# P x V of a macaron block: the two array halves take one head each, and ScalarE alone empties the banks

## The reference

```
scores = jnp.einsum('bqhd,bkhd->bhqk', q_full, k_full) * softmax_scale
causal = jnp.tril(jnp.ones((S, S), dtype=bool))
scores = jnp.where(causal[None, None], scores, jnp.finfo(scores.dtype).min)
attn = jax.nn.softmax(scores, axis=-1)
out = jnp.einsum('bhqk,bkhd->bqhd', attn, v).reshape(B, S, H * VD)
return out @ wo.T
```

## Time and profile before

| what | value |
|---|---|
| runs | 1891.0, 1892.49, 1895.84 us (median 1892.49) |
| profiled execution, span | 1895.1 us |
| TensorE busy | 1803.7 us, 95% |
| VectorE busy | 1231.4 us, 65% |
| ScalarE busy | 1000.5 us, 53% |
| GpSimd busy | 877.8 us, 46% |
| attention's P x V (L1307) | first at 386.6 us, last at 1332.0 us |

### The profile page before, as it was taken

One profiled execution on the slowest core, in us unless ns is written; L12 is line 12 of the kernel. 1 busy time (PEld: TensorE's weight loads), 2 busy tenths in 40 slices (PEclk: granted clock), 3 DMA queues, 4 the chain that ended last, 5 costly groups with the idle time before them and its releaser, 6 DMA issues. The chain is left out here.

```text
span 1895.1 us, 44298 instructions
## 1 busy us (share of the span) xinstructions
PE 1803.7 (95%) x15472; PEld 1422.9 (75%) x15472; DVE 1231.4 (65%) x2654; ACT 1000.5 (53%) x2137; POOL 877.8 (46%) x641
## 2 busy tenths in 40 slices
PE   5999969899999999999999999998999999989999
PEld 4788869877777777777777777775788888877887
DVE  5655358688898888889888888989521111125453
ACT  2221047788887888888787888877310100112110
POOL 3232112377777878777787878775000000014321
PEclk9999979999999999999999999999999999989999
DMA  6542162311212112121222212123742233224321
GB/s 217 193 156 100 67 173 94 84 62 44 86 59 78 57 62 80 57 80 40 85 69 68 69 51 82 55 86 113 249 151 89 94 100 115 67 87 158 130 89 59
DMA packets 111969, 182.74 MB, mean 96 GB/s; under 512 B 27680, under 2 KB 64672, under 8 KB 109856
## 3 DMA queue, kind: packets, MB, share of 16 engines
q1 hardware_dynamic: 111904, 181.88, 29.8%
HBM read 122.33 MB, written 59.51 MB: 96 GB/s over the span
## 5 line engine op out<-in xcount | busy, mean ns | idle before, releaser
L1290 PE MATMUL psS<-keyT,q 128*128 128x512 f32 (+2 forms) x2304 | 473.2, 350 | 23.9 <-POOL q L648 14.5
L1290 PEld LDWEIGHTS psS<-keyT,q 128*128 128x128 f32 x2304 | 381.2, 189 | 118.2 <-DVE negmax L1408 41.7
L1357 ACT ACTIVATE prob<-prob,negmax 128x640 f32<-128x640 f32 (+7 forms) x512 | 392.0, 767 | 78.5 <-DVE negmax L1408 75.9
L1418 DVE STREAM_TRANSPOSE pT<-prob 128x640 f32<-128x640 f32 (+7 forms) x512 | 379.9, 762 | 66.4 <-PE psV L1307 61.6
L1408 DVE CUSTOM_DVE_ANT_0 prob<-psS,mask 128x640 f32<-128x640 f32 (+7 forms) x512 | 371.9, 742 | 20.9 <-PE psS L1290 7.4
L469 PE MATMUL f_psy<-f_weff,f_xT 128*128 128x512 f32 x1344 | 315.6, 393 | 0.0
L1101 PE MATMUL psS<-o_w,o_o 128*128 128x512 f32 x1344 | 304.8, 389 | 0.0
L469 PEld LDWEIGHTS f_psy<-f_weff,f_xT 128*128 128x128 f32 x1344 | 250.9, 188 | 55.8
L1101 PEld LDWEIGHTS psS<-o_w,o_o 128*128 128x128 f32 x1344 | 252.3, 188 | 52.4
L1307 PE MATMUL psV<-pT,val 32*64 32x512 f32 (+3 forms) x8192 | 264.8, 407 | 6.4 <-DVE pT L1418 6.2
L1307 PEld LDWEIGHTS psV<-pT,val 32*64 32x64 f32 x8192 | 168.8, 132 | 109.7 <-issue 66.2
(11 more groups left out here) (120 smaller groups left out, 1919.1 us busy)
## 6 DMA issues: line engine op xcount, KB each, us to landing
wo<-in_wo SPq DMA_DIRECT2D x16, 1024.0 KB, 6.0
pT<-row_scales SPq DMA_DIRECT2D x128, 128.0 KB, 2.9
oT<-pT SPq DMA_DIRECT2D x64, 256.0 KB, 2.5
o_in<-oT SPq DMA_DIRECT2D x32, 512.0 KB, 5.2
f_xt<-in_x SPq DMA_DIRECT2D x16, 512.0 KB, 4.4
f_w_in<-in_w SPq DMA_DIRECT2D x16, 512.0 KB, 6.7
w_sum<-f_w_in SPq DMA_DIRECT2D x16, 512.0 KB, 5.3
x<-f_xo SPq DMA_DIRECT2D x16, 512.0 KB, 3.0
```

The lines of the kernel that those rows point to most:

```text
L1290: ins = nc.tensor.matmul(psS[:, slot, start + x0:start + x1], q[:, e, a, t * P:(t + 1) * P], k.keyT[:, m, b * S + x0:b * S + x1], start=(i ...
L1357: nc.scalar.activation(row, row, ACT.Exp, bias=negmax[:, n % 8:n % 8 + 1], scale=-1.0, accum_out=rowsum[:, column(n, s):column(n, s) + 1]) ...
L1418: nc.vector.transpose(pT[:, n % 2, t, 0:width], prob[:, n % RING, 0:width]).then_inc(turned, 1)
```

## The change

TensorE: the two column halves now take the two heads (index e), and each half walks through all four key blocks. A matmul streams one head only, up to 8 x 32 = 256 columns, and there are 256 matmuls in a step instead of 128; each weight block is now loaded once for each head. The number of columns that each of the eight tiles streams is the same. A bank now holds finished sums, head 0 on partitions 0 to 63 and head 1 on 64 to 127, in 256 columns.

ScalarE: one copy of 128x256 per bank writes `o_raw` itself and raises `evicted`; it takes over the wait for the stores of the step before.

VectorE: the four O jobs are gone from `DVE_STEP`, the semaphore `copied` is gone, and the last round's `weights_lo` is one run over all 16 pairs.

```diff
-            "T6+0 R0+0 T7+0 O0-1 M8+0 O1-1 F0+0 M9+0 O2-1 T8+0 F1+0 M10+0 M11+0 T9+0 O3-1 M12+0 M13+0 T10+0 T11+0 "
+            "T6+0 R0+0 T7+0 M8+0 F0+0 M9+0 T8+0 F1+0 M10+0 M11+0 T9+0 M12+0 M13+0 T10+0 T11+0 "
...
-        def upper(bank):
-
-            return (cosT, sinT)[bank // 2][0:KVR, bank % 2 * BANK:(bank % 2 + 1) * BANK]
+        def of_block(bank):
+
+            return bank[:, 0:32 * QT].rearrange("p (t r) -> p t r", r=32)
...
-                for a in range(BLOCKS // 2):
-                    for half in range(2):
+                for block in range(BLOCKS):
+                    for e in range(2):
                         for i in range(BLOCKS):
-                            rows, block = slice(32 * i, 32 * i + 32), BLOCKS // 2 * half + a
-                            x = kt * P + 32 * block
-                            out = psV[KVR * half:KVR * half + KVR, i, :].rearrange("p (e t r) -> p e t r", e=2, r=32)
-                            ins = nc.tensor.matmul(out[:, :, kt:QT, :], val[rows, b, block, kt, :], pT[rows, :, kt:QT, x:x + 32],
-                                                   start=(kt == 0 and a == 0), stop=(kt == QT - 1 and a == BLOCKS // 2 - 1))
+                            rows, x = slice(32 * i, 32 * i + 32), kt * P + 32 * block
+                            out = of_block(psV[KVR * e:KVR * e + KVR, i, :])
+                            ins = nc.tensor.matmul(out[:, kt:QT, :], val[rows, b, block, kt, :], pT[rows, e, kt:QT, x:x + 32],
+                                                   start=(kt == 0 and block == 0), stop=(kt == QT - 1 and block == BLOCKS - 1))
...
                 if later(step, 1):
-                    act.wait_ge(evicted, step * 4 + bank - 3)
-                nc.scalar.activation(upper(bank), psV[KVR:P, bank, :], ACT.Copy).then_inc(copied, 1)
+                    for ch in range(2):
+                        act.wait_ge(o_stored[ch], step * 16)
+                nc.scalar.activation(by_block(o_raw, bank), of_block(psV[:, bank, :]).rearrange("p (h t) r -> p h t r", h=2),
+                                     ACT.Copy).then_inc(evicted, 1)
...
-                dve.wait_ge(copied, step * 4 + bank + 1)
...
-                    ins = nc.vector.tensor_tensor(by_block(o_raw, bank)[KVR * e:KVR * e + KVR], halves[0], halves[1], ALU.add)
-                ins.then_inc(evicted, 1)
...
-                        if r.last and s == 1 and n == 0:
-                            output.weights_lo(nc, dve, range(2 * SLOTS))
-                        join_values(r.it, n, s)
...
-            output.weights_lo(nc, dve, range(2 * SLOTS, PAIRS))
+            output.weights_lo(nc, dve, range(PAIRS))
```

More of the change, by code:

```diff
@@ L1134, in attention_phase @@
         r_stored, r_loaded = c.sem("r_stored"), [c.sem(f"r_loaded{ch}") for ch in range(2)]
-        valued, copied, evicted, scaled = c.sem("valued"), c.sem("copied"), c.sem("evicted"), c.sem("scaled")
+        valued, evicted, scaled = c.sem("valued"), c.sem("evicted"), c.sem("scaled")
         o_stored = [c.sem(f"o_stored{ch}") for ch in range(2)]
@@ L1431, in row_scales @@
                 nc.vector.transpose(rinvT[:, x // QT, :], rinv[:]).then_inc(r_turned, 1)
-            def join_values(it, bank, s):
-                step = it * 2 + s
-                dve.wait_ge(copied, step * 4 + bank + 1)
[L1437 to L1442, removed]
-                    ins = nc.vector.tensor_tensor(by_block(o_raw, bank)[KVR * e:KVR * e + KVR], halves[0], halves[1], ALU.add)
-                ins.then_inc(evicted, 1)
             nc.vector.memset(rinv[:], 1.0).then_inc(zeroed, 1)
@@ L1456, in body @@
                         row_scales(r.it, n, s)
-                    elif job == "O":
-                        if r.last and s == 1 and n == 0:
-                            output.weights_lo(nc, dve, range(2 * SLOTS))
-                        join_values(r.it, n, s)
                     elif job == "F":
```

## The result

The changed kernel takes 2218.5 us (median of 4 runs, 2201.8 to 2224.7), the kernel before in the same session 1893.6 (1891.0 to 1895.8): 1.170 times as long (95% interval 1.165 to 1.175). Forecast were 1930 us and at most 1960. The direction was right. The size was wrong by 288 us, nearly all of the loss.

The account below looks back on a forecast made before the run. TensorE, busy 95% of the span, was taken as the bound almost everywhere. 1895.1 us, plus 15 (26.0 - 3 - 3.1 - 4.5), plus 23 for refetched code, gave 1933 against the profiled span, so 1930 us; range 1898 to 1960.

Parts of the forecast that it names:

- Pace of the pairs: TensorE's P x V: each pair of weight load and matmul takes at least 14.5 ns, making P x V 1.4 us longer.
- the floor: TensorE's P x V: a least time per pair, 14.5 ns, so 0.93 us for the 64 pairs of a narrow key tile.
- The reading of kt 7: Old trace's narrowest key tile: 0.61 us, some 0.2 of it the last matmul's way, leaving 12.5 ns a pair.
- The forecast that kt 4 to 7 would be alike: The four narrow key tiles of P x V: each takes 0.85 to 1.0 us, whatever its columns.
- Waits behind P x V vanish: TensorE's waits on GpSimd and VectorE right behind P x V: mean 0.6 us a step, absorbed by the longer P x V.
- VectorE, ScalarE and the last steps: Joins gone: 3 us gained over the steps, 3.1 in the last two steps, 4.5 behind the last P x V.
- The new wait of ScalarE for the stores: ScalarE's copy waits for the stores of the step before: costs nothing; up to 2.5 us a step if uncovered.
- The body doesn't stay in the store: TensorE's loop body, grown to 2465 records, over ten packets, is fetched again at returns; held likelier than that it fits.
- Price of a return: TensorE's loop head, right behind P x V: 1.8 us per refetch, 13 returns, 23 us; range 1.0 to 3.5 a return.
- Packets inside P x V: TensorE's P x V: forecast 9.3 to 9.9 us long, with some 150 instruction packets on q8 in the run.
- rival 3: Fetches inside P x V on demand only: two steps lose 14 us more, the kernel passes 2100 us; chance 0.05.
- Rival 2: P x V grows only 0.1 us, swallowed by the waits behind it: 1885 us; not slower below 0.9 us growth; chance 0.1.

Follow-up runs that it names:

- experiment 6: The kernel before with only its last 1, 2, 4 or 5 key tiles written one head at a time: 1898.2, 2000.5, 2105.4, 2161.9 us.
- Experiment 2: The kernel before with ScalarE copying whole 128x256 banks and VectorE joining nothing, TensorE untouched, some sums and columns left out: 1883.4 us, ratio 0.994.
- Experiments 3: The kernel before with two rounds written out in TensorE's loop body, 2977 records, seven passes in place of 14: 1944.9 us, ratio 1.026.
- experiment 4: The changed kernel with TensorE's 16 rounds written out, so without any return to a loop head: 2151.1 us, ratio 1.139 against the kernel before.
- Experiment 5: The kernel before with TensorE's 16 rounds written out, so without any return to a loop head: 1897.7 us, ratio 1.0017.
- experiment 7: P x V of key tiles kt 0 to 3 left out of the changed kernel and of the kernel before: 1955.5 and 1957.5 us.

## Why the prediction was wrong, point by point

**Pace of the pairs (14.5 ns, +1.4 us per P x V): too high, and not what counted.** With the code at hand 64 pairs take 0.65 to 0.70 us where the floor gave 0.93, and the four narrow tiles grow by 0.68 us where 1.4 was forecast (3.71 + 0.25 against the 2.57 of the earlier trace rows). The reading of kt 7 was sound: the trace has 0.22 us for the last matmul's way, as allowed, and so some 12.5 ns a pair. The step from there up to 14.5 failed, the argument that a long run of narrow parts has less queued: four such parts on end go at 14.7, 12.3, 10.9 and 10.2 ns, the later the faster. The forecast that kt 4 to 7 would be alike fell as well: 0.94, 0.79, 0.70, 0.65.

**Waits behind P x V vanish (0.6 us): right, though a P x V as long as this one makes it certain.** In the changed kernel's list of waits TensorE has one on GpSimd left, of 0.5 us, where before there were 44 with 14.5 us. With one tile apart (experiment 6) P x V grows by 0.29 us (first to last start 8.28 against 7.99) and the kernel by only 4 us, 0.13 a step: the waits took the other half, so at a small growth not all of the 0.6 us comes back.

**VectorE, ScalarE and the last steps (-3 and -7.6 us): right by themselves, nothing of it in the changed kernel.** Experiment 2 carries them alone. From the second P x V to the one before the last it gains 3.9 us over 29 steps, 0.14 a step against 0.1. The last step gave 1.6 where 3.1 was forecast, and behind the last P x V 6.6 us where 4.5 was. The terms forecast add up to 10.6 and the median moved by 10.3; two of them missed by half in opposite directions, so that match is partly luck. In the changed kernel 573.7 us follow the start of the last P x V, before they were 573.0: two waits for packets inside it, 5.5 us, took its place. The new wait of ScalarE for the stores cost nothing, and its copy takes 389 ns:

```profile
L1372 ACT ACTIVATE pT<-psV 128x256 f32<-128x256 f32 x128 | 38.8, 389 | 231.5 <-PE psV L1306 231.5
```

The row gave 382. The 231.5 us of idle time ahead of it show the copies now waiting for P x V, so nothing of ScalarE is on the path.

**The body doesn't stay in the store: right**, and the sentence "nothing says that the store is much larger than what it was seen to hold" bore it out. The edge lies between 1617 and 1745 records. (The 2465 records of the prediction are matmuls and weight loads alone; the body has 2513.) The Trainium skill, "Runtime: NRT & Kernel Launch", section "Instruction fetch mechanics", gives TensorE 2048 instructions, refilled first in, first out. By it alone 1745 and 2001 records would stay, and experiment 6 does not agree: 42 packets against 98 put the edge lower. Whether the store is smaller, or a part of it goes to what is read past the loop's end, no run tells.

**Price of a return (1.8 us, bounds 1.0 to 3.5): mis-sized, the first failed term.** The wait is 4.3 us in the mean (56.1 / 13), beyond the upper bound. It was built from a small DMA's way and the packet's own transfer. It also lacks the half clock behind the wait, which doubles it. A return costs 8.1 to 8.3 us, 13 of them about 107 us where 23 were forecast. The earlier trace rows had shown a clock of 0.89 behind a wait of 4.35 us, and that was used for the tail and not here.

**Packets inside P x V: the second failed step, and the larger.** P x V should have taken 9.3 to 9.9 us and q8 some 150 packets; they are 12.7 to 18.6 us, 15.1 in the median, and 209. It stood as rival 3 with a chance of 0.05, and at 1.8 us a packet it gave over 2100. What was wrong is the picture behind it: that the body once missing comes as a stream which runs well ahead, so that only the jump is paid. The stream holds about one packet ahead and brings one per 4 us, so P x V waited 144 us for packets in all. The first P x V of the changed kernel, ahead of any return, already shows it:

```profile
385.75 6.11 PE L1306 MATMUL psV<-pT,val 32*64 32x256 f32 x266 [0.20 <-issue]
392.95 1.95 PE L1306 MATMUL psV<-pT,val 32*64 32x128 f32 x128 [1.10 <-issue]
396.96 1.45 PE L1306 MATMUL psV<-pT,val 32*64 32x64 f32 x118 [2.05 <-issue]
```

The trace of before could not show the rate, since its P x V of two packets in 8.21 us never asked for more; but rival 3's own arithmetic, one packet per 2.4 us against an unknown rate, should have had the same chance as the refetch itself. Experiments 3 and 4 split the loss: 257 us are there without any return (4), and the returns add 67 on top, less than their 107, since part of the waiting and of the half clock is there already.

The same section of the Trainium skill says that the cost of crossing a 16 KiB boundary is mostly hidden. Experiment 5 agrees with that (1.0017 with over 70 crossings more) and experiment 4 does not (waits of 0.6 to 2.1 us at the three crossings shown, 3.6 us the longest). What decides is how long 256 records last.

**What the change would be worth with its code at hand** is an estimate: 31 x 0.68 us from P x V, less what the waits give back, 0.6 us a step as forecast or only half of the growth as in experiment 6, is +4 to +10 us. With -10.3 us from the evictions it would be between 7 us faster and no faster than before. No run has all of P x V one head at a time in a body that stays; a loop over single steps was not tried. Rival 2 of the prediction had this mechanism, and its point of decision at 0.9 us stands above the measured growth.

## What to carry to other kernels

Count the records of TensorE's program before halving its matmuls. On this chip a loop of 1617 records stayed and one of 1745 came again at 8 us and more per pass, and any stretch that works off 256 records that aren't at hand in less than some 4 us waits for the next packet, loop or not. A wide matmul is worth more than its columns: it buys time for the instructions behind it. And a wait of 4 us cost about 8 here, because TensorE came back at half its clock.

## What the runs showed of the hardware that was not expected

- Instruction packets that TensorE waited for came 3.5 to 5.4 us apart in the changed kernel, 4.0 in the median, with little more than two packets (266 pairs) at hand even after TensorE had waited 6 us. Written out in full, the kernel before is only 1.0017 times as long.
- The longest body that stays over a loop's return is between 1617 and 1745 records, and the step at that edge is 102 us for 14 passes. Bodies of 2001 records and more fetched some two packets a pass beyond their own size.
- Less work made the kernel slower. With 5.6 us of P x V taken out of each step the time rose by 3.4%, at a mean granted clock of 0.92 instead of 0.99. P x V had been filling the time in which TensorE otherwise waits for GpSimd (14.5 us of such waits before, 170.6 without it).
- Pairs of weight load and matmul on eight tiles of the array, 32x64 each, follow each other every 10 to 11 ns at the narrow end (kt 6 and 7, experiment 7).
